# Another order of the second half in a fused attention and feed-forward kernel: gate, products and additions without a break, two query tiles and two value blocks first

## The reference

```python
x = L0_attn_x                                    # (16, 512, 256), float32
q, k, v = split(x @ qkv_w + qkv_b)               # 16 heads of 16
local = softmax(mask(q @ k.T / 4)) @ v           # window: the 128 tokens before, own one left out
pooled = x.reshape(B, 64, 8, 256).mean(2)        # 64 latent tokens
rq = x @ rq_w + rq_b; rk, rv = split(pooled @ rkv_w + rkv_b)
remote = softmax(mask(rq @ rk.T / 4)) @ rv @ rout_w + rout_b     # 4 latent heads
gate = sigmoid(local @ gl_w + remote @ gr_w)     # per head
mixed = gate * local + (1 - gate) * remote
x = layernorm(x + mixed @ out_w + out_b)
h = gelu(rmsnorm(x) @ ternary(w_up).T)           # 1024 wide
x = layernorm(x + rmsnorm(h) @ ternary(w_down).T)
```

## Time and profile before

| | |
|---|---|
| median of three runs | 1356.45 us |
| the profiled execution | 1356.7 us, span of the trace 1354.9 us |
| PE busy | 1125.0 us (83%), mean granted clock 0.916 of full speed |
| DVE busy | 1026.3 us (76%) |
| POOL busy | 708.1 us (52%) |
| ACT busy | 671.9 us (50%) |
| DMA, mean rate | 79 GB/s |

### The profile page before, as it was taken

The page is one execution under the profiler, slowest core; times in us unless marked ns, Lnnn a source line. Parts: engine busy times, 40 slices in busy tenths (PEclk is TensorE's granted clock), DMA queues, the critical chain, the costliest instruction groups (busy, mean ns, idle before and its releaser), DMA issues.

```text
span 1354.9 us, 31716 instructions
## 1 busy us (share of the span) xinstructions
PE 1125.0 (83%) x12704; PEld 690.3 (51%) x12704; DVE 1026.3 (76%) x2048; ACT 671.9 (50%) x1024; POOL 708.1 (52%) x866
## 2 busy tenths in 40 slices
PE   4667989897998989897987989798888989785855
PEld 2334545564655556464654555465555545454433
DVE  7755777878877787888787886888787687876566
ACT  2113455564646546464646555464655545462624
POOL 6413546473644636473654646374563647364643
PEclk9676989899988989899999999899898889997877
DMA  6984190846639192754729093663919275471000
GB/s 167 120 111 64 51 124 21 120 70 97 78 85 106 34 124 53 107 82 84 91 68 122 20 128 62 98 76 84 106 45 114 52 104 79 86 80 34 1 16 16
DMA packets 114482, 107.68 MB, mean 79 GB/s; under 512 B 13312, under 2 KB 113792, under 8 KB 114304
## 3 DMA queue, kind: packets, MB, share of 16 engines
q1 hardware_dynamic: 114336, 105.65, 52.2%
HBM read 71.55 MB, written 34.08 MB: 78 GB/s over the span
## 4 chain that ended last, share of the span: by engine, by line
PE 39%; DMA 21%; DVE 20%; SPq 6%; POOL 5%; issue 5%; ACT 3%; DVEq 0%; POOLq 0%
DMA Ks<-parts_scratch 18%; PE oacc L1372 7%; PE work L1321 7%; PE scores L1354 7%; SPq L446 3%; DMA parts_scratch<-parts 3%; DVE x L1035 3%; PE work L1382 3%; SPq L449 2%; DVE x L1043 2%; PE work L1444 2%; PE work L1203 2%; PE work L1326 2%; POOL parts L573 2%; DVE nmax L977 2%
## 5 line engine op out<-in xcount | busy, mean ns | idle before, releaser
L743 ACT ACTIVATE Pt<-scores 128x1024 f32<-128x1024 f32 (+1 forms) x256 | 231.8, 914 | 157.9 <-PE oacc L1372 94.6
L609 POOL TENSOR_TENSOR h_lo<-hbuf,h_hi 128x512 f16<-128x512 f32 x128 | 175.4, 1372 | 239.6 <-DVE h_hi L1088 239.6
L977 DVE TENSOR_REDUCE nmax<-work 128x3 f32<-128x480 f32 x352 | 217.5, 637 | 68.4 <-PE work L1326 64.1
L581 POOL TENSOR_SCALAR_AFFINE_SELECT Pt<-Pt 128x512 f32<-128x512 f32 x256 | 163.3, 638 | 130.4 <-ACT Pt L743 129.5
L1444 PE MATMUL work<-xnT,wup_t 128*128 128x512 f16 x512 | 151.6, 432 | 32.1 <-DVE xnT L1079 32.1
L1321 PE MATMUL work<-Ks,Qs 98*32 98x160 bf16 x4096 | 139.1, 243 | 39.1 <-DMA Ks<-parts_scratch 21.5
L1354 PE MATMUL scores<-Qs,Ks 100*128 100x256 bf16 (+1 forms) x1024 | 144.1, 267 | 3.1 <-ACT Pt L743 1.8
L1372 PE MATMUL oacc<-Pt,Vp 128*32 128x256 f32 (+1 forms) x2048 | 144.9, 360 | 1.9 <-POOL Pt L585 1.8
L1321 PEld LDWEIGHTS work<-Ks,Qs 98*32 98x32 bf16 x4096 | 77.2, 98 | 102.4 <-issue 40.9
L1093 DVE TENSOR_TENSOR oT<-oT,hsq 128x512 f32<-128x512 f32 x112 | 121.5, 1085 | 10.0 <-ACT hsq L784 10.0
L1228 PE MATMUL scores<-xT,wqk 128*128 128x512 f32 x256 | 116.3, 608 | 13.4 <-ACT xT L678 13.4
(11 more groups left out here) (166 smaller groups left out, 2082.0 us busy)
## 6 DMA issues: line engine op xcount, KB each, us to landing
parts_scratch<-parts SPq DMA_DIRECT2D x48, 512.0 KB, 3.0
Qs<-parts_scratch SPq DMA_DIRECT2D x96, 256.0 KB, 14.7
Ks<-parts_scratch SPq DMA_DIRECT2D x96, 256.0 KB, 16.5
xtok<-L_attn_x SPq DMA_DIRECT2D x16, 512.0 KB, 22.4
xres<-L_attn_x SPq DMA_DIRECT2D x16, 512.0 KB, 21.7
y<-ytok SPq DMA_DIRECT2D x16, 512.0 KB, 3.0
Qs<-L_ffn_w_up SPq DMA_DIRECT2D x1, 1024.0 KB, 7.0
Qs<-L_ffn_w_down SPq DMA_DIRECT2D x1, 1024.0 KB, 8.2
```

The costliest lines, as they stand in the source:

```text
L581: ins = pool.affine_select(out=pt[:, :, 0:P], in_=pt[:, :, 0:P], compare_op=ALU.is_gt, fill=0.0, base=0, pattern=[[0, 4], [1, P]], channel ...
L609: pool.tensor_tensor(h_lo[:, t % NR, :], hbuf[:, t % 2, :], h_hi[:, t % NR, :], ALU.subtract).then_inc(h_lo_ready, 1)
L743: nc.scalar.activation(Pt[:, u % NPT, :, 0:w], scores[:, slot, :, :].rearrange("p k (h q) -> p (k h) q", h=2)[:, :, 0:w], ACT.Exp, scale=S ...
L977: nc.vector.tensor_reduce(nmax[:, :, :].rearrange("p b h -> p (b h)")[:, first:first + n], work[:, slot, 0:n * BAND].rearrange("p (h c) -> ...
```

## The change

`SECOND_HALF` gets another order. MIX comes right behind GATE. QK, QK+1, VALUES and VALUES+1 come next, then MIX_T, QK+2, OUT, QK+3 and LAT_IN. `P_ORDER`, and with it the rotation of the PSUM banks, follows. DVE walks a second tuple, `VECTOR_HALF`, which has NORM ahead of LAT_IN, VALUES+2 and LAT_SCORES. PE, ACT and POOL walk `SECOND_HALF`. DVE's pooling sum (L904) moves from the step QK to the step QK+2.

```diff
 SECOND_HALF = (
-    ("P", X_T), ("F", GATE), ("P", QK), ("F", MIX), ("P", QK + 1), ("P", QK + 2), ("P", QK + 3),
-    ("F", MIX_T), ("P", LAT_IN), ("F", OUT), ("P", VALUES), ("P", VALUES + 1), ("P", LAT_SCORES),
-    ("F", NORM), ("P", LAT_SCORES + 1), ("P", VALUES + 2), ("P", VALUES + 3), ("F", XN_T),
-    ("P", LAT_NORM), ("F", UP), ("F", UP + 1), ("P", LAT_T), ("F", UP + 2), ("P", LAT_T + 1),
+    ("P", X_T), ("F", GATE), ("F", MIX), ("P", QK), ("P", QK + 1), ("P", VALUES), ("P", VALUES + 1),
+    ("F", MIX_T), ("P", QK + 2), ("F", OUT), ("P", QK + 3), ("P", LAT_IN), ("P", VALUES + 2),
+    ("P", LAT_SCORES), ("F", NORM), ("P", LAT_SCORES + 1), ("F", XN_T), ("P", VALUES + 3),
+    ("F", UP), ("P", LAT_NORM), ("F", UP + 1), ("P", LAT_T), ("F", UP + 2), ("P", LAT_T + 1),
     ("F", UP + 3), ("P", LAT_O), ("F", UP + 4), ("P", REMOTE), ("F", UP + 5), ("P", REMOTE + 1),
     ("F", UP + 6), ("F", UP + 7), ("F", END))
+VECTOR_HALF = (
+    ("P", X_T), ("F", GATE), ("F", MIX), ("P", QK), ("P", QK + 1), ("P", VALUES), ("P", VALUES + 1),
+    ("F", MIX_T), ("P", QK + 2), ("F", OUT), ("P", QK + 3), ("F", NORM), ("P", LAT_IN), ("P", VALUES + 2),
+    ("P", LAT_SCORES), ("P", LAT_SCORES + 1), ("F", XN_T), ("P", VALUES + 3),
+    ("F", UP), ("P", LAT_NORM), ("F", UP + 1), ("P", LAT_T), ("F", UP + 2), ("P", LAT_T + 1),
...
@@ p_step of DVE
-                if k == QK:
+                if k == QK + 2:
                     for t in range(KT):
                         bank, n = p_use(s, t)
                         dve.wait_ge(p_taken[bank], n + 1)
@@ body of DVE
-                for phase, k in SECOND_HALF:
+                for phase, k in VECTOR_HALF:
```

More of the change, by code:

```diff
@@ L72 @@
 SECOND_HALF = (
-    ("P", X_T), ("F", GATE), ("P", QK), ("F", MIX), ("P", QK + 1), ("P", QK + 2), ("P", QK + 3),
-    ("F", MIX_T), ("P", LAT_IN), ("F", OUT), ("P", VALUES), ("P", VALUES + 1), ("P", LAT_SCORES),
-    ("F", NORM), ("P", LAT_SCORES + 1), ("P", VALUES + 2), ("P", VALUES + 3), ("F", XN_T),
-    ("P", LAT_NORM), ("F", UP), ("F", UP + 1), ("P", LAT_T), ("F", UP + 2), ("P", LAT_T + 1),
+    ("P", X_T), ("F", GATE), ("F", MIX), ("P", QK), ("P", QK + 1), ("P", VALUES), ("P", VALUES + 1),
+    ("F", MIX_T), ("P", QK + 2), ("F", OUT), ("P", QK + 3), ("P", LAT_IN), ("P", VALUES + 2),
+    ("P", LAT_SCORES), ("F", NORM), ("P", LAT_SCORES + 1), ("F", XN_T), ("P", VALUES + 3),
+    ("F", UP), ("P", LAT_NORM), ("F", UP + 1), ("P", LAT_T), ("F", UP + 2), ("P", LAT_T + 1),
     ("F", UP + 3), ("P", LAT_O), ("F", UP + 4), ("P", REMOTE), ("F", UP + 5), ("P", REMOTE + 1),
     ("F", UP + 6), ("F", UP + 7), ("F", END))
+VECTOR_HALF = (
[3 more added lines that the diff above has]
+    ("F", UP), ("P", LAT_NORM), ("F", UP + 1), ("P", LAT_T), ("F", UP + 2), ("P", LAT_T + 1),
+    ("F", UP + 3), ("P", LAT_O), ("F", UP + 4), ("P", REMOTE), ("F", UP + 5), ("P", REMOTE + 1),
+    ("F", UP + 6), ("F", UP + 7), ("F", END))
+assert sorted(VECTOR_HALF) == sorted(SECOND_HALF)
 STEPS_P = [k for phase, k in SECOND_HALF if phase == "P"]
```

## The result

The changed kernel takes 1458.2 us, the median of four runs between 1455.91 and 1463.4, against 1354.09 us for the kernel before in the same session. The ratio is 1.078, with a 95% interval of 1.0731 to 1.0829. The forecast was 1445 us, 6.5% slower. Direction and size are right, the size in part by luck: the stacks, on which the forecast rests, are not what PE waits for, and a term that was taken as nothing fills the place.

A forecast was written before the change was run, and what follows sets the result against it. Bound: the stacks' trip through DRAM, closely matched with the engines' work. 14 stacks, each 6.4 us later, less 1 us of slack in two cases, make 88 us on 1356.7 us: 1445 us, range 1408 to 1475.

The forecast's parts named there:

- What bounds the kernel before: Stacks' trip through DRAM, closely matched with the engines' work: stacks last in 12 of 14 cases, by 1.8 us on the mean.
- The additions and OUT: DVE's four additions follow the products at once, taking 2.38 us, a gain of 1.8 us for MIX_T; OUT starts 2.7 us earlier.
- The new wait of QK+2 for its bank: On PE, QK+2 takes QK's PSUM bank, which the first rest frees at 698.7, so it runs 698.75 to 700.55.
- POOL's queue: OUT's power waits behind the third tile's part 2, the last part 2 behind the power: last part ready 6.4 us later.
- The third rival: POOL's order holds up the last part less: ready 4.2 us late instead of 6.4, 1414 us; chance 0.12.
- The trip: From the last part on POOL through DRAM to PE's first max_scores: 36.6 us, taken as unchanged, with -1.5 us as a bound.
- The tail up to UP: LAT_IN behind NORM on DVE: PE idles 5.6 us ahead of LAT_SCORES, and XN_T starts 5.5 us late.
- The tail behind UP: UP and all behind it are late by the same 5.5 us, so the tail stays ahead of the stacks by 3.9 us.
- The clock: PE's lower clock after the wait for the stacks: between nothing and 1.7 us per sequence, taken as nothing.
- first rival: The tail decides: low clock after PE's idle 5.6 us ahead of LAT_SCORES costs up to 4.9 us, 1458 us; chance 0.15.
- The second, the clock behind the stacks: Stacks stay last and each wait costs 1.7 us of clock on top: 22 us more, 1467 us; chance 0.16.
- Faster: Stacks only seemingly last, xn not held up: body shorter by OUT's 2.7 us earlier start, 1319 us; chance 0.04.

The follow-up runs named there:

- e5_before_loads_by_part: The kernel before, with each part's stacks read back once that part has landed in DRAM, instead of all twelve loads after all three parts; 1314.76 us, ratio 0.9725.
- e1_one_order: The changed kernel with DVE walking SECOND_HALF like the other engines instead of VECTOR_HALF; 1441.73 us, ratio 1.0659.
- e2_fill_gap: The changed kernel with value block VALUES+2 multiplied six times instead of once, to fill PE's idle time ahead of LAT_SCORES; 1417.73 us, ratio 1.0492.
- e4_tiles_early: The changed kernel with QK+2 and QK+3 right behind QK+1 again, ahead of VALUES, VALUES+1, MIX_T and OUT; 1418.1 us, ratio 1.0487.
- e10_tiles_early_one_order: e4_tiles_early with DVE walking SECOND_HALF too; 1389.07 us, ratio 1.0311.

## Why the prediction was right, and where it was not

The forecast was 13 us low, and that is in part luck. Its path was the stacks, at 60.2 us after X_T; they land at 56.9. The path that decides is the tail, for which it had 56.3; it stands at 61.0. Two errors of 3 to 5 us against each other leave 0.8 us between the forecast and the first `max_scores` of body 7.

**What bounds the kernel before: right.** e5_before_loads_by_part shows it from outside the trace.

**The additions and OUT: right in direction, too small.** OUT's products start 12.0 us after X_T, forecast 12.7. The additions were taken at 2.38 us for four from rows 5. In the new place they took 1.73 us, up to 747.01:

```profile
745.28 1.73 DVE L1053 TENSOR_TENSOR x<-x,rem 128x256 f32<-128x256 f32 x4
```

**The new wait of QK+2 for its bank: right.** `747.73` in the chain above is QK+2, directly behind the first rest.

**POOL's queue: right.** The variance is ready at 755.48, but the power starts only behind the third tile's part, and the fourth part behind the power:

```profile
756.21 1.16 POOL L583 TENSOR_TENSOR parts<-Pt,parts 128x512 bf16<-128x512 f32 x1 [4.01 <-ACT parts L703]
757.32 1.65 POOL L611 TENSOR_TENSOR rs<-rs,power 128x8 f32<-128x8 f32 x1
758.93 1.15 POOL L583 TENSOR_TENSOR parts<-Pt,parts 128x512 bf16<-128x512 f32 x1
```

The last part is 5.3 us late, forecast 6.4; 0.7 of the 1.1 us are there already at OUT's start. The third rival (a queue that costs less) is out.

**The trip, taken as unchanged: mis-sized.** The prediction took 36.6 us from body 7, whose stacks came later than most: the mean from the last part to the last landing was 35.8 us before and is 34.4 us in the changed kernel. It had 1.5 us less as a bound. The stacks are 53.0 us after X_T on the mean before and 57.2 us now, so they are later by 4.2 us, not 6.4. Where nothing hides them, in e1_one_order, they arrive at 57.2 to 59.7. The same body gave the tail too much room: its wait of 2.98 us made the margin 3.9 us, and with the mean wait, 21.5 / 14 = 1.5 us, it would have been 2.4.

**The tail up to UP: right, and UP's place partly by luck.** LAT_SCORES, XN_T and UP are within 0.8 us of the forecast. But e2_fill_gap, at full clock, has XN_T at 30.0 and UP at 33.0: the order costs 1.0 and 1.6 us less than forecast, and the low clock behind the gap, which the forecast left out, brings 1.2 and 1.5 us. The idle PE ahead of LAT_SCORES, told as 5.6 us, is 5.96:

```profile
763.49 2.08 PE L1270 MATMUL scores<-lat_bd,rqT 64*128 64x256 f32 x8 [5.96 <-DVE lat_bd L942]
```

**The tail behind UP: the step that failed.** The sentence was "UP and all behind it are late by the same". It holds only if nothing behind UP is moved, and LAT_NORM is. DVE's 3 us of normalisation (717.39 to 720.35 in body 7) came ahead of UP's cast in the kernel before. Now DVE stands idle for 1.68 us ahead of that cast, waiting for ACT, and the normalisation comes behind it (774.84 to 777.81), so that PE waits at LAT_T:

```profile
777.87 1.11 PE L1296 MATMUL scores<-ident,Pt 128*128 128x128 f32 x4 [3.17 <-DVE Pt L973]
```

The step cost little by itself: with it the tail at full clock would stand at about 55.9 us by the estimate above, against the forecast 56.3, as UP would come 1.6 us earlier than forecast. That is about even with the stacks at 56.9.

**The clock, taken as nothing: the term that was mis-sized.** It falls in the gap ahead of LAT_SCORES in every body (0.69 in the 5 us from LAT_SCORES on in body 8, 0.50 in body 2). With that fall alone the tail stands at 57.7 to 57.9 (bodies 1 and 2), and is last by 1.2 us already, as the stacks land at 56.5 there. In bodies 3 to 13 the clock is low again behind LAT_T (0.50). In bodies 5 to 13 that lifts the tail by another 3.2 us, to 61.0. For its sum the prediction weighed only the clock behind the wait for the stacks, at 0 to 1.7 us, and took nothing; the clock behind the gap is in its first rival alone. The clock ahead of the first `max_scores` is worth 61.0 - 55.9 = 5.1 us a body by the same estimate.

**The rivals.** The first, the tail decides, is what happened. It had 0.15, and its 1458 us is the measured time, but partly by luck: it put a loss of 4.9 us on LAT_SCORES, XN_T, VALUES+3 and the first UP products. Up to UP the low clock costs 1.5 us (34.5 against 33.0 in e2_fill_gap), and the larger share lies behind UP. The second, the clock behind the stacks, is e1_one_order. "Faster" got its small chance for the right reason: of the 3.4 us by which OUT starts earlier, 1.7 are left at POOL's power (19.7 against 21.4), and LAT_IN behind NORM gives back more than those. The Trainium skill, "TensorE: Matmul & The Clock Gate", "HAM oscillation — how this bites in real kernels", says that idle gaps of PE bring its clock down. That agrees with the gap of 6.0 us, which is followed by a low clock in all 14 bodies, and with e2_fill_gap, where filling it won 40 us. Not every gap is paid: behind the wait of 3.2 us at LAT_T bodies 1 and 2 keep the full clock.

## What to carry to other kernels

Where two paths end within 2 us of each other, as the stacks and the tail did, price both to their ends before naming the bound, and go through every line of a reordered list, the last one too: the smallest swap (LAT_NORM by one place) was worth 18 us alone and 43 to 46 us under a tail that was last. Read such paths in more than one body: body 7 was one of the latest for the stacks. A wait of PE can cost its length and then the work behind it at the lower clock, so filling it with useless products can pay, and an order of its own for one engine only helps if what the other engines have queued ahead of its result (here the latent exponential ahead of `xn` on ACT) is not pushed back by it. The gain that came without moving any step was to start each load when its own part is there.

## What the hardware showed that I had not expected

The same waits cost the clock in one body and not in the next. e4_tiles_early and the changed kernel have a gap of 5.0 and 6.0 us ahead of LAT_SCORES and the same 3.2 us at LAT_T, LAT_SCORES to UP at the same times after X_T, and yet differ by 3.4 us behind it, where one has the full clock and the other 0.50. Bodies 2 and 8 of the changed kernel differ in the same way with gaps that are equal. Each kernel settles: from body 5 on the changed kernel repeats every 85.3 us with the clock low at the same places, and e4_tiles_early and e2_fill_gap, with quite different falls of the clock, both repeat every 81.9 us. In e10_tiles_early_one_order the first `max_scores` comes at 54.9 and 56.8 us strictly in turn. What decides between the two cases in a given body was not tried, beyond filling the first gap.

DVE instructions took longer where a POOL instruction ran beside them. `lat_bd` takes 425 ns in the changed kernel, and took 1153 ns (both medians of 16) in the kernel before, where it ran beside the last part on POOL. In the changed kernel the first small instruction of NORM took 1.10 us instead of 0.15, from 759.00 to 760.10, beside POOL's last part from 758.93 to 760.08. Which operations are stretched and why was not separated.
